# z projected in pieces of two channel tiles by half the tokens, paired transpositions, DMA-transposed FFN input

## The reference

```
zxbcdt = u @ in_proj_w.T ;  z, xBC, dt = split(...)        # z: 1024, x: 1024, B and C: 128 each, dt: 64 heads
x, B, C = silu(conv4(xBC)) ;  dt = softplus(dt + bias)
y = chunked_scan(x, dt, A, B, C) + x * D                   # chunks of 64 tokens, state carried from chunk to chunk
yg = y * silu(z) ;  yn = yg * rsqrt(mean(yg^2)) * w ;  x1 = layernorm(u + yn @ out_proj_w.T)
h = silu(x1 @ gate.T) * (x1 @ up.T) ;  out = layernorm(x1 + (h @ down.T) / rms)
```

## Time and profile before

| | us |
|---|---|
| median of 3 runs | 1715.55 (1709.31 to 1716.58) |
| profiled execution | 1714.83, span 1713.0 |
| prologue (to the first dt of a block) | 118 |
| one block (dt to dt) | 132.9 |
| FFN, 1154 to 1710 | 556 |

### The profile page before, as it was taken

The page is one execution under the profiler, slowest core; times in us unless marked ns, Lnnn a source line. Parts: engine busy times, 40 slices in busy tenths (PEclk is TensorE's granted clock), DMA queues, the critical chain, the costliest instruction groups (busy, mean ns, idle before and its releaser), DMA issues.

```text
span 1713.0 us, 39037 instructions
## 1 busy us (share of the span) xinstructions
PE 1570.0 (92%) x14272; PEld 769.6 (45%) x14272; DVE 1328.7 (78%) x2018; ACT 907.1 (53%) x1585; POOL 1103.8 (64%) x1085
## 2 busy tenths in 40 slices
PE   2789999999989999999999997878999999999998
PEld 1245445445445445444444444433444444444443
DVE  5759868968968968977977987967777777777774
ACT  2654454364455445545445445328666666666662
POOL 0348728828838937837846855748777767767773
PEclk9899999999999999999999999989999999999999
DMA  7031151142142133124124018320010110111101
GB/s 237 5 102 31 29 133 39 25 116 60 22 106 62 29 83 88 26 65 110 25 60 117 20 50 244 60 67 26 25 58 30 62 51 32 54 39 48 34 29 62
DMA packets 214764, 109.80 MB, mean 64 GB/s; under 512 B 133876, under 2 KB 185776, under 8 KB 214576
## 3 DMA queue, kind: packets, MB, share of 16 engines
q1 hardware_dynamic: 214576, 107.37, 23.8%
HBM read 80.57 MB, written 26.76 MB: 63 GB/s over the span
## 4 chain that ended last, share of the span: by engine, by line
PE 68%; DVE 14%; issue 6%; ACT 6%; POOL 2%; DMA 1%; SPq 1%; DVEq 0%; ACTq 0%; POOLq 0%
PE ps_in L781 17%; PE ps_in L941 8%; PE ps_in L803 8%; PE ps_yo L956 7%; PE ps_yd L956 7%; PE ps_s L941 4%; PE ps_t L941 4%; DVE pre L1293 4%; PE ps_yd L855 3%; PE ps_yo L867 2%; PE ps_d L843 2%; PE ps_s L880 2%; PE ps_t L828 2%; ACT decay L1089 1%; DVE dte L1329 1%
## 5 line engine op out<-in xcount | busy, mean ns | idle before, releaser
L1089 ACT ACTIVATE decay<-ps_d 128x512 f32<-128x512 f32 x256 | 149.3, 592 | 239.5 <-PE ps_d L843 173.4
L1710 POOL TENSOR_TENSOR xend<-xpad,decay 128x256 f32<-128x256 f32 x256 | 211.6, 848 | 65.5 <-PE ps_yo L880 43.7
L781 PE MATMUL ps_in<-u_hi,w_hi 128*128 128x512 f16 x576 | 221.5, 384 | 30.7 <-DVE pre L1293 16.2
L803 PE MATMUL ps_in<-w_out,zg 128*128 128x512 f32 x512 | 231.5, 606 | 0.9
L781 PE MATMUL ps_in<-u_lo,w_hi 128*128 128x512 f16 x576 | 220.6, 383 | 0.0
L781 PE MATMUL ps_in<-u_hi,w_lo 128*128 128x512 f16 x576 | 220.5, 383 | 0.0
L1381 DVE TENSOR_TENSOR mix<-decay,gb 128x1024 f32<-128x1024 f32 x128 | 196.6, 1536 | 17.3 <-ACT decay L1089 16.3
L1818 POOL TENSOR_TENSOR gate_sum<-gate_sum,gate_part 128x512 f32<-128x512 f32 x88 | 142.2, 1616 | 102.8 <-DVE gate_part L1631 102.4
L1293 DVE SCALAR_TENSOR_TENSOR pre<-ps_in,cws,pre 128x511 f32<-128x511 f32 (+2 forms) x240 | 178.9, 746 | 28.7 <-ACT pre L1029 23.0
L803 PEld LDWEIGHTS ps_in<-w_out,zg 128*128 128x128 f32 x512 | 96.3, 193 | 132.9 <-issue 132.9
L941 PE MATMUL ps_in<-xt_hi,gu_w 128*128 128x512 f16 x352 | 133.9, 380 | 7.0 <-DVE gate_sum L1631 2.5
(11 more groups left out here) (194 smaller groups left out, 3750.4 us busy)
## 6 DMA issues: line engine op xcount, KB each, us to landing
ebc<-e_dram SPq DMA_DIRECT2D x256, 64.0 KB, 2.8
u<-u_t SPq DMA_DIRECT2D x9, 1024.0 KB, 5.8
res<-u_tok SPq DMA_DIRECT2D x32, 256.0 KB, 3.4
x_dram<-res SPq DMA_DIRECT2D x32, 256.0 KB, 2.2
xa<-x_dram SPq DMA_DIRECT2D x8, 1024.0 KB, 5.7
xr<-x_dram SPq DMA_DIRECT2D x32, 256.0 KB, 2.6
out<-xr SPq DMA_DIRECT2D x32, 256.0 KB, 2.0
fw_words<-gu_words SPq DMA_DIRECT2D x32, 176.0 KB, 4.1
```

The costliest lines, as they stand in the source:

```text
L781: last = mm(ps_in[bk][:, :], w[:, k, col:col + P], u[:, k, :], start=(k == 0 and j == 0), stop=(k == KT - 1 and j == 2))
L803: last = mm(ps_in[bk][:, :], zg[:, k, tt * P:(tt + 1) * P], w_out[:, k, :], start=(k == 0), stop=(k == CT - 1))
L1089: ac(decay[:, n % NG, :, :].rearrange("p a b -> p (a b)"), ps_d[n % 2][:, :], ACT.Exp).then_inc(e_done, 1)
L1710: g_.tensor_tensor(xend[:, pairs, :], xpad[:, c % 2, pairs, :], decay[:, g, :, CH - 1:CH].broadcast_to([P, CT, 2 * HD]), ALU.mult).then_in ...
```

## The change

- z is projected in eight pieces Z0 to Z7. A piece is two channel tiles by half the tokens: 24 matmuls on 256 columns into one bank. Z0 to Z3 are the first half of the tokens, Z4 to Z7 the second. Z0, Z1, Z2 stand in slots 22, 24, 26, Z3 in the tail before o3, Z4 and Z5 between a0, e0, a1, e1 and e2, Z6 and Z7 in slots 0 and 1 of the scan they are for. `scale_u` moves from slot 0 to the end of slot 1, `split_hi` and `split_lo` to 2 and 3, since Z6 and Z7 still read u.
- dt moves from slot 4 to 5, B from 5 to 6, C from 7 to 8, x5 from 27 to 30; the dt parts from 7 and 20 to 8 and 22, the third step from 22 to 24.
- xs is laid out by chunk, so a transposition takes two channel tiles (128 columns): four in place of eight. B is kept doubled in b2 and C in cc: one matmul and one transposition in place of four instructions. aux has two steps in place of three. silu_all has four operations, x first.
- The FFN input of rows 1 to 7 is split first by ACT and DVE, by tokens (xh16, xl16), and transposed by eight DMAs a period that SP issues. PE's turn and its PSUM banks are used for row 0 alone.

```diff
-HEAD = ["a0", "z1", "z2", "e0", "a1", "e1", "z3", "a2", "e2", "z4", "z5", "z6", "z7"]
-PRO_ORDER = ["dt", "B", "C", "x0", "x1", "x2", "x3", "x4", "z0", "x5", "z1", "x6", "z2"]
-TAIL = {"pro": ["x7", "z3", "z4", "a0", "z5", "z6", "z7", "e0", "a1", "e1", "a2", "e2"], "body": ["x6", "x7", "z0", "o3", "q3"] + HEAD, "last": ["o3", "q3"]}
+HEAD = ["a0", "e0", "Z4", "a1", "e1", "Z5", "e2"]
+PRO_ORDER = ["dt", "B", "C", "x0", "x1", "x2", "x3", "x4", "Z0", "x5", "Z1", "x6", "Z4"]
+TAIL = {"pro": ["x7", "Z5", "Z2", "a0", "Z3", "e0", "a1", "e1", "e2"], "body": ["x6", "x7", "Z3", "o3", "q3"] + HEAD, "last": ["o3", "q3"]}
-BODY_USES = [(4, "dt"), (5, "B"), (7, "C"), (9, "x0"), (11, "x1"), (12, "o0"), (13, "q0"), (17, "x2"), (19, "x3"),
-             (20, "o1"), (21, "q1"), (25, "x4"), (27, "x5"), (28, "o2"), (29, "q2")]
+BODY_USES = [(0, "Z6"), (1, "Z7"), (5, "dt"), (6, "B"), (8, "C"), (9, "x0"), (11, "x1"), (12, "o0"), (13, "q0"), (17, "x2"),
+             (19, "x3"), (20, "o1"), (21, "q1"), (22, "Z0"), (24, "Z1"), (25, "x4"), (26, "Z2"), (28, "o2"), (29, "q2"), (30, "x5")]
...
+                if name[0] == "Z":
+                    half, pair = divmod(int(name[1]), CT // 2)
+                    t = slice(half * LH, (half + 1) * LH)
+                    for i in range(2):
+                        col = Z_COL + (2 * pair + i) * P
+                        for k in range(KT):
+                            for j, (w, u) in enumerate(passes):
+                                last = mm(ps_in[bk][:, i * LH:(i + 1) * LH], w[:, k, col:col + P], u[:, k, t],
+                                          start=(k == 0 and j == 0), stop=(k == KT - 1 and j == 2))
...
-                    for k in range(4):
-                        last = tr(ps_t[0:CH, k * P:(k + 1) * P], xs[:, 4 * use + k, t], ident[:, :])
+                    for k in range(CT // 2):
+                        last = tr(ps_t[:, k * P:(k + 1) * P], xs[:, c, 2 * k * CH:2 * (k + 1) * CH], ident[:, :])
...
+                    mm(ps_t[:, 0:CH], b2[:, c, :], cc[:, c, :], start=True, stop=True)
+                    last = tr(ps_t[:, CH:CH + NS], b2[:, c, :], ident[:, :])
...
+            def turn(f, par):
+                need(sp, gu_full, (f - 1) * UNITS)
+                settled(sp)
+                for t in range(TT):
+                    sp.wait_ge(half_hi, (f - 1) * TT + t + 1)
+                    settled(sp)
+                    sp.dma_start_transpose(xt_hi[par][:, :, t * P:(t + 1) * P], xh16[:, t, :]).then_inc(xt_in, 16)
+                    sp.wait_ge(half_lo, (f - 1) * TT + t + 1)
+                    settled(sp)
+                    sp.dma_start_transpose(xt_lo[par][:, :, t * P:(t + 1) * P], xl16[:, t, :]).then_inc(xt_in, 16)
```

More of the change, by code:

```diff
@@ L99, in banks_of @@
     names = [name for _, name in uses]
-    turned = names.index("q2") + 1 if "q2" in names else len(uses)
-    return [(i + (i >= turned)) % 2 for i in range(len(uses))]
+    return [(i + sum(n in ("q1", "q2") for n in names[:i])) % 2 for i in range(len(names))]
 class Stage:
@@ L129, in before, with z_free @@
         return Stage("pro", 0) if isinstance(self.scan, int) and self.scan == 0 else Stage("body", self.scan - 1)
+    def z_free(self, half):
+        counts = {}
+        for name in Z_HALF[half]:
+            held = self if name in ("Z6", "Z7") else self.before()
+            bk, _, full = held.bank(name)
+            counts[bk] = max(counts.get(bk, 0), full)
+        return sorted(counts.items())
     def last_z(self):
-        found = [self.bank(f"z{i}") for i in (CT - 2, CT - 1)]
+        found = [self.bank(name) for name in ("Z6", "Z7")]
         assert found[0][0] != found[1][0]
@@ L614, in room_free @@
             def room_free(last):
-                for bk, full in last.before().last_z():
+                for bk, full in last.last_z():
                     sp.wait_ge(in_full[bk], full)
-                sp.wait_ge(silu_done, nb * 3)
+                sp.wait_ge(silu_done, nb * SILUS)
                 sp.wait_ge(u_max, nb + 1)
@@ L989, in _, with split_hi @@
             ac = nc.scalar.activation
-            def split_hi(b, before, tiles):
+            def split_hi(b, st, tiles):
                 act.wait_ge(u_scale, (b + 1) * 5)
-                if before is not None:
-                    for bk, count in before.last_z():
+                if st is not None:
+                    for bk, count in st.last_z():
                         act.wait_ge(in_full[bk], count)
@@ L1046, in take_z @@
                 act.wait_ge(in_full[bk], full)
[L1047 removed]
+                half, pair = divmod(int(name[1]), CT // 2)
+                if st.kind == "pro" and name == "Z0":
                     act.wait_ge(w_lo_done, KT * len(W_BLOCKS))
[L1049 to L1050 removed]
+                if st.kind == "body" and name in ("Z0", "Z4"):
+                    ob, _, ofull = st.bank("o1" if name == "Z0" else "o3")
                     act.wait_ge(in_full[ob], ofull)
[L1052 to L1053 removed]
+                    act.wait_ge(sq_done, st.scan * NC + (half + 1) * NC // 2)
+                ac(zg[:, 2 * pair:2 * pair + 2, half * LH:(half + 1) * LH], ps_in[bk][:, :].rearrange("p (k t) -> p k t", k=2),
+                   ACT.Silu, scale=uundo[:, 0:1]).then_inc(in_free[bk], 1)
             def use_in(st, slot):
@@ L1492, in body @@
                     c, g = n // NG, n % NG
-                    if n == 0 and st.proj is not None:
-                        scale_u(st.proj, st.before())
                     if g == 0 and c > 0:
@@ L1523, in body @@
                         decode(b, k, part)
+                    if n == 1 and st.proj is not None:
+                        scale_u(st.proj, st)
                 y_all(b, NC - 1)
```

208 lines of the change are left out of this document (111 added, 97 removed).

## The result

The changed kernel takes 1790.1 us (median of 4 runs, 1783.7 to 1795.1) against 1715.6 us, ratio 1.0437 [1.0418, 1.0457]: slower, as forecast, by 74.6 us where 46 were forecast (1762). Its profiled execution spans 1786.5 us, 73.5 more than the 1713.0 of before.

A forecast was written before the change was run, and what follows sets the result against it. PE was taken as the bound in both stages, by its work plus pauses. Seven blocks at +8.4 us (+59), prologue and last block +1 and FFN -12 made +48 on 1714.83, forecasting 1762 us, range 1700 to 1795.

The forecast's parts named there:

- e2: An exponent step of the scan in the block's head, not a run: PE was forecast to wait 0.5 us for it.
- The likeliest case of the forecast: Whole kernel: slower, 1762 us, as ACT and POOL set the head and x6 waits in the tail; chance 0.59.
- Tail: End of o2 to end of o3: +7.4 us a block from x5's work, x6's wait and low clock (bounds +5.3, +9).
- The walk: Step-by-step timing of a block's parts; in the tail it starts x6 at 611.65 and ends o3 at 627.2, not 620.8.
- Head: End of o3 to slot 6's start, 37.7 us: removed z projections buy nothing, 0 us a block (bounds -3.3, +2).
- Middle: Slot 6's start to end of o2, 76.8 us: slot 23's pause goes, new bank waits come, +1 (bounds -3, +3).
- Transpositions: PE work per chunk in the blocks: 0.75 us for 1.37, 0.62 saved (bounds 0.4 and 0.8).
- Prologue: Ahead of the first scan, summed with the last block: +1 us for both (0 to +2).
- FFN: Seven periods lose four groups of PE transpositions each, DMA transposes hidden: -12 us (bounds -12.3 and +190).
- rival C: FFN: DMA transposes are slow, PE waits at the periods' start; at 9 us each 1895 us; chance 0.05.
- Rival D: ACT: a table switch costs another 1.4 us beyond its load, say 5 us a block, 1797 us; chance 0.03.
- Rivals A and B: Whole kernel: A, faster, PE stays the bound, 1677 us, chance 0.22; B, no change, 1717 us, chance 0.11.

The follow-up runs named there:

- e3_no_reduce: e1_out_first with GpSimd's maximum of |u| over the partitions left out, a two-column add in its place: 1755.5 us, ratio 1.0239.
- e1_out_first: The changed kernel with one DVE order turned: an out projection's take_out is issued before the previous slot's convolution taps (matters in slot 31): 1758.8 us, ratio 1.0266.
- e5_pairs_only: The kernel before the change with only the paired transpositions (four a chunk for eight), z and FFN as before: 1712.4 us, ratio 0.9988.
- e4_ffn_only: The kernel before the change with only the FFN input's split in token layout and DMA transposes, blocks unchanged: 1706.6 us, ratio 0.9955.
- e8_grouped: e1_out_first with ACT's head grouped by table: Z4 and Z5 before the first exponent, Z6 moved to slot 1 beside Z7: 1758.0 us, ratio 1.0247.
- e6_pairs_ffn: The kernel before the change with paired transpositions and the FFN's DMA transposes, z as before: 1702.2 us, ratio 0.9928.
- e7_pieces_old_places: The changed kernel with z's eight half-token pieces at the old tiles' places, dt again in slot 4: 1702.2 us, ratio 0.9930.

## Why the prediction was right in sign and 28 us short

The likeliest case of the forecast, "the three removed projections buy nothing: ACT and POOL set the head", with a tail that waits for take_out(2), is what happened. e3_no_reduce adds that POOL is not alone in it: without its reduction DVE's mix holds the same exponent to within 2 us. Step by step:

- **Tail: right.** Forecast +7.4 a block, of it 3.8 of waiting and 1 for the clock. Measured 24.9 against 18.5 us, +6.4, in regular blocks, and up to +9.4 where the clock fell (0.68 granted around 648.45, that is, part of it at 1.2 GHz). The wait is 3.3 us, seven times. e1_out_first took 31.3 us away where the prediction's 3.8 + 1, seven times, would be 34. (The walk's own times put x6 6.8 us later, 0.4 more than its terms of 2.6 and 3.8.) A pause of 3.3 us did not lower the clock in each block, so "+1 in every block" was in truth about 0 in four and 1.3 to 3 in three.
- **Head: the mechanism was right, its size 2 us short.** The walk gave PE a wait of 5.7 us for e5 at slot 4; it is 5.79. The shorter waits for e1, e2 and the copies (forecast 1.6, 0.5 and 1.7 us) are 1.49, 0.55 and 1.54. But I let ACT load the table for e4 while it waited for POOL. It loads it after the wait (688.34), 1.3 us later, and in this block POOL's first tensor operation comes 19.4 us after the end of o3 and not 18.9. The low clock behind the wait, which I had in the upper bound alone, is there in all seven heads: PE's exponent at 697.05 takes 0.61 us where the one at 675.47 takes 0.39. In the regular block from 231.64, PE's exponent behind the wait comes 29.3 us after the end of o3 for a forecast 28.2, and dt 33.8 for 31.8. Measured 39.5 to 40.0 against 37.7 us, at my upper bound of +2.
- **Middle: right within 1.** Forecast +1, measured 78.5 against 76.8. The waits at x1 (0.7 to 1.4 for 1.0), Z0 (1.2 for 0.7), Z1 (1.2 for 1.9) and the aux of slot 25 (1.5 for 0.9) are there; the one at x2 for take_out(0) (1.2) is not, and one of 0.7 for xpad is new. The pause of slot 23 on mix is gone from the regular blocks.
- **Transpositions: right as work, not as time.** PE's work fell as forecast (four in 0.44 us; 38 us of busy time in e5_pairs_only), and I booked -3.1 us a block of it in the middle. On the old schedule e5_pairs_only shows that it comes back as waits and a lower clock, 0.9988. In the changed kernel it can't be told apart from the rest of the middle; that sum is 0.7 us off.
- **Irregular blocks, +10.3 us: not forecast.** Three of seven blocks are longer than the regular ones, by the clock behind the pause and in one by a stop of 2.45 us in the slots after the head. e1_out_first keeps a rest of that (pitch 139.7 regular, one of 142.6), so the pause is most of it.
- **Prologue, +4.2 for +1.** I counted its pieces but didn't walk it: the first scan has the head's wait as well (5.79 us before the exponent at 118.03), and less work ahead of it than before.
- **FFN: -7.1 for -12.** The transfers are hidden, rival C is out: each lands in 2.4 us and occupies SP's queue for 1.2. e4_ffn_only has the same stretch at 563.3 us, so the 7 us are this part's and not the last block's. What came back: PE's idle time between the last o3 and the end grew by 3.7 us (19.7 to 23.4, from the windows), 1.5 of it in the first period, where four waits for DVE and ACT of 0.9 to 1.9 us appear, and 2.1 spread over the six others; and PE's busy time fell by 10.8 us and not by 12.3. From one period's first gate_up to the next, a regular period went from 68.2 to between 66.9 and 67.1 us, 1.1 to 1.3 for the 1.76 of the turns; the 64 to 65 that I named rested on a period of 66 that was wrong. The DMA page of the kernel after (us to landing):

```profile
xt_hi<-xh SPq DMA_TRANSPOSE x28, 2.4
xt_lo<-xl SPq DMA_TRANSPOSE x28, 2.4
```

- **Rival D is out.** 118 changed tables at L1137 and L1099 took 1283 ns each, the instruction behind one follows within 0.02 us in the timeline above, and e8_grouped removed 44 with 0.8 us of gain. The Trainium skill (ScalarE: Activation LUTs, What ACT_TABLE_LOAD costs) is borne out in the load of 1283 ns and not in the drain of about 1380 ns.
- **Rivals A and B are out** as stated: both had a head 3.3 us shorter, and it is longer; PE didn't stay the bound. Rival A's thought survives: with z at the old places the same parts give 1702.

In sum: the first block and six at the regular pitch +66.8 for the forecast 58.8, irregular blocks +10.3 for 0, prologue +4.2 for under 1, last scan -0.7, FFN -7.1 for -12. (The forecast's own sum is 1762.8.) All terms but the tail and the last scan came out dearer than forecast, and the time lies 5 us inside a range whose upper end is 33 us above the forecast: the mechanism was no luck, but staying in the range with an unforecast term of 10.3 us owes something to its width.

The price list, by medians, leads from 1715.6 to 1790: pairs, DMA transposes and the form of z together -13, later slots 2 at most, moved pieces of z +54.5, order in DVE's slot 31 +31.3. It adds up by construction, since each kernel is a step from the one before it; what it shows is the size of the steps.

## What to carry to other kernels

Work that sits beside a latency which other engines set is cover, even if the page calls its engine the bound: before moving it, ask what PE will do in its place, and expect no gain there from less PE work. Look for the instruction order within a slot on every engine that frees a bank (one swap of two lines was worth 31 us). And when several queues are ready at about the same time, removing one shows only the next: price a chain by giving its cover back, as here, or by removing its members together, which no run here tried.

## What the runs showed of the hardware

- A projection of 24 matmuls on 256 columns runs at the pace of 12 on 512 (a start every 0.11 us for every 0.22; e6_pairs_ffn and e7_pieces_old_places: 1702.2 us both), and four float32 transpositions of 128 x 128 take what four of 128 x 64 take, 0.44 us.
- GpSimd's reduction over partitions of a 128x1 column has a record of 0.38 us, but 8.0 us go by before it and 7.2 us between it and GpSimd's next tensor operation (678.84 and 686.39).
- In these kernels ScalarE's table load runs behind the semaphore wait of the activation that needs it (1.28 us after 5.10 us of waiting, and likewise in the seven other heads), not under it.
- A DMA transposition of 128 KB in 16 bits between places in SBUF takes 1.2 us of SP's queue to issue and lands in 2.4 us; with 56 of them PE's idle time in a regular period of the FFN is 0.1 to 0.3 us.
- A pause of TensorE of 3.3 us was followed by the lower clock in three blocks of seven, one of 5.1 to 5.8 us in all seven (the first matmul behind it takes 0.61 us in place of 0.39).
